# Two-layer vision kernel: image 0's first routing at earlier attention steps, routings that choose on logits, band matrices built by VectorE

## The chip, the cores and the metric

The kernel runs on one core of one Trainium2 chip. The metric is the time of the device in microseconds (us) for the whole program. A core has five engines that run their own queues in order: TensorE (PE, with its weight loads as PEld), VectorE (DVE), ScalarE (ACT), GpSimd (POOL) and SyncE (SP), which here only issues DMAs. They meet through semaphores.

## The reference

Two images of 48 x 48 tokens with 128 channels go through two layers. What the change touches are the two routings and one convolution:

```
# layer 0
x = x + window_attention(ln_c(x))        # 8 heads, windows of 4x4 queries, 8x8 keys
t = ln_t(tokens(x))
probs = softmax(t @ router_w.T)          # 8 experts
rw, re = top_k(probs, 2); rw = rw / max(sum(rw), 1e-12)
t = t + (t + sum_e combine[:, e] * (gelu(t @ w1[e] + b1[e]) @ w2[e] + b2[e]))
# layer 1
h = group_norm(conv1x1(ln_c(x)))         # 32 channels
y  = conv over channels, 9 taps (2..8 masked in) ; y2 = depthwise 9x9 conv, central 7x7
z = relu(group_norm(y + y2)); z = relu(group_norm(conv1x1(z))) + input
t = ln_t(tokens(z)); probs = softmax(t @ gate_w + gate_b)   # 16 experts
top 2 normalised by their sum; out = t_in + sum of the two experts' silu(x w1) * (x w2) @ w3
```

Because the two chosen probabilities are divided by their sum, the gates are 1 / (1 + e) and e / (1 + e), with e the exponential of second minus first logit.

## The kernel before

Each image is 18 tiles of 128 tokens, in six groups of three. One list, `order`, is written by hand, and every engine runs from it, in its order, the phases that it has a part in (`run`). `beside(kind, first, last, pieces)` lays a loop of steps and puts pieces behind numbered steps ("marks"); pieces of one mark stand in the order of the list given.

**Attention** is `("A", n)` for n from 0 to 55: 48 half window rows (24 per image) and eight steps to drain the pipeline. In step n PE makes the scores of n + 1 (line 671), transposes the probabilities of n - 3 (682), weighs n - 4 (695) and, in odd steps, projects n - 6 (706). VectorE adds the bias and takes maxima of n (1215, 1217) and sums of n - 1 (1221, 1225); GpSimd subtracts maxima of n (580), normalises n - 2 (589) and spreads queries of n + 2 (571); ScalarE takes the exponential of n - 1 (971), copies transposed probabilities of n - 3 (982) and outputs (990, 995). Behind marks stand the attended groups of each image (`YA`: transposed by PE on line 325, added by VectorE on line 1237; `YS`: their statistics), and image 0's first routing: `LN`, `SQ`, `LV` (statistics, square root, coefficients), six groups `LT` normalised by ScalarE (947), six groups `RT` transposed by PE and evacuated by ScalarE (953), `LG` logits (733), `RC` the choice in pieces 0 to 5 on VectorE, `RE` an exponential on ScalarE, `RX` the combine rows (PE 766, VectorE 1329). Inside attention all of `YA`, `RT`, `LG`, `RX` use bank 0 in turn: each waits until the one before is read.

After attention `TO` runs on GpSimd: 12 products that spread the 9x9 taps into matrices (549), 13 small operations for the channel taps (552 to 560). SyncE stores the combine rows to DRAM, reads them back, and broadcasts them as gates, four experts of a group at a time (lines 464 to 475).

**The dense layer** 0 is `("D", n)`, n from 0 to 99: 12 groups x 8 experts. Step n is a hidden product on PE (781), gelu on ScalarE (1021), the product with the gate on GpSimd (615) and, four steps later, the second product on PE (798). The second half also holds image 0's layer 1 convolution, taps on line 902, for which the matrices must be there from mark 71.

**Layer 1 routings** `RC` with l = 1 are in the list behind the logits of each image. VectorE subtracts the maximum (1263, 1264), ScalarE takes the exponential (1013), VectorE normalises (1274 to 1276), chooses twice (1280 to 1286). Then PE multiplies the chosen flags by a triangular and an all-ones matrix (810, 811), VectorE computes each token's slot (`slots`, 1358 to 1395), and GpSimd scatters the rows, 36 indirect DMAs per image (632). `moe(0)` works 20 tiles of 128 rows of image 0, `moe(1)` the other 68, after image 1's scatter (827, 836, 847). `KW` are matmuls only for the PE clock (867).

## Time and profile before

| | us |
|---|---|
| median of 3 runs (lowest to highest) | 683.85 (678.06 to 684.36) |
| the profiled execution | 683.36 |
| its span | 681.3 |
| PE busy, share | 554.9, 81% |
| VectorE | 348.6, 51% |
| ScalarE | 342.1, 50% |
| GpSimd | 408.2, 60% |
| mean granted TensorE clock | 0.905 |

The chain that ended last is 56% PE, 14% VectorE, 9% GpSimd, 9% issue, 7% ScalarE and 3% DMA. Times in the rows further down are from the start of the span. Attention runs from about 50 to 185 us, the dense layer to about 380, convolution and routings to 510, the experts of layer 1 to 658, the last sums and stores to the end. A mean over all this says little on a change to one stage: what ends a wait in that stage has to be read there.

### The profile page before, as it was taken

The numbers are of one execution on the slowest core, as the hardware profiler recorded it, in microseconds if no ns is written. First come the engines' busy times: TensorE is split into PE (matmuls) and PEld (weight loads), VectorE is DVE, ScalarE is ACT, GpSimd is POOL, SyncE is SP. The second block draws the span as 40 slices with busy tenths as digits, with TensorE's granted clock in tenths as the row PEclk, the third lists the DMA queues.
The fourth block names the chain that finished last, engine by engine and source line by source line (L and its number), as shares of the span: only waits on it lengthen the run. The fifth ranks groups of instructions, "written<-read, shape, count | busy, mean of one in ns | idle before, by whom it ended". The sixth has DMA issues, their size and how long they took to land.

```text
span 681.3 us, 15719 instructions
## 1 busy us (share of the span) xinstructions
PE 554.9 (81%) x5422; PEld 468.6 (69%) x5423; DVE 348.6 (51%) x1021; ACT 342.1 (50%) x801; POOL 408.2 (60%) x468
## 2 busy tenths in 40 slices
PE   2477788778779999999999999959649729999960
PEld 2466667657547777677777678748639729999960
DVE  6977787846620171212001274784875405555563
ACT  4467668886547243674122552522515406666640
POOL 1568789767567388675333330037747777777771
PEclk9689999979869699999999988978978959999995
DMA  8452322212055455322219200001123123333457
GB/s 296 161 140 82 85 73 81 67 47 70 13 180 201 154 174 171 128 94 99 88 47 331 61 1 1 0 23 52 52 61 98 52 85 99 98 97 98 128 204 242
DMA packets 56288, 72.15 MB, mean 106 GB/s; under 512 B 9086, under 2 KB 46934, under 8 KB 55614
## 3 DMA queue, kind: packets, MB, share of 16 engines
q1 hardware_dynamic: 49374, 58.36, 27.5%
q0 software_dynamic: 5120, 10.57, 4.7%
q10 hardware_dynamic: 1728, 2.36, 0.9%
q8 instruction: 39, 0.64, 0.4%
q14 instruction: 27, 0.22, 0.1%
HBM read 55.83 MB, written 21.69 MB: 114 GB/s over the span
## 4 chain that ended last, share of the span: by engine, by line
PE 56%; DVE 14%; POOL 9%; issue 9%; ACT 7%; DMA 3%; SPq 1%; POOLq 0%; DVEq 0%; ACTq 0%
PE bank L836 12%; PE bank L798 9%; PE bank L781 8%; PE bank L902 7%; PE bank L847 6%; POOL gathered_or_att L580 3%; POOL padded_or_w L571 3%; ACT normed L947 2%; POOL gathered_or_att L589 2%; PE bank L325 2%; DVE ln_stats L1133 2%; PE bank L796 2%; PE bank L827 2%; PE bank L733 2%; PE bank L867 1%
## 5 line engine op out<-in xcount | busy, mean ns | idle before, releaser
L615 POOL TENSOR_TENSOR padded_or_w<-padded_or_w,gathered_or_att 128x384 f32<-128x384 f32 x96 | 95.4, 1000 | 80.7 <-ACT padded_or_w L1021 77.0
L632 POOL DMA_INDIRECT sorted_x<-normed,slot x72 | 71.2, 989 | 80.0 <-DVE slot L1395 51.4
L1021 ACT ACTIVATE padded_or_w<-bank,moe_b 128x384 f32<-128x384 f32 x96 | 55.3, 579 | 107.2 <-PE bank L781 107.1
L651 POOL DMA_INDIRECT returned<-gathered_or_att,home_of_slot x88 | 87.2, 991 | 26.8 <-issue 19.8
L798 PEld LDWEIGHTS bank<-moe_or_conv,padded_or_w 128*128 128x128 f32 x576 | 80.6, 197 | 30.9 <-issue 9.8
L798 PE MATMUL bank<-moe_or_conv,padded_or_w 128*128 128x128 f32 x576 | 83.9, 284 | 0.0
L781 PE MATMUL bank<-chan_major,moe_or_conv 128*128 128x384 f32 x192 | 82.7, 517 | 0.1
L671 PE MATMUL bank<-padded_or_w 64*64 64x64 f32 x1152 | 47.5, 233 | 27.3 <-issue 15.9
L1459 DVE TENSOR_TENSOR att_or_moe<-att_or_moe,bank 128x256 f32<-128x256 f32 x88 | 37.0, 420 | 61.2 <-ACT att_or_moe L1035 39.9
L671 PEld LDWEIGHTS bank<-padded_or_w 64*64 64x64 f32 x1152 | 41.5, 145 | 36.6 <-issue 32.8
L580 POOL TENSOR_TENSOR gathered_or_att<-gathered_or_att,score_max 128x384 f32<-128x384 f32 x48 | 39.9, 830 | 34.5 <-DVE score_max L1217 33.7
L1035 ACT ACTIVATE att_or_moe<-bank 128x256 f32<-128x256 f32 x88 | 33.7, 383 | 50.7 <-PE bank L836 50.7
L1342 DVE TENSOR_TENSOR residual<-residual,bank 128x384 f32<-128x384 f32 x12 | 6.6, 552 | 98.6 <-PE bank L798 98.6
L982 ACT ACTIVATE gathered_or_att<-bank 64x384 f32<-64x384 f32 x96 | 46.2, 481 | 19.9 <-PE bank L682 19.3
L836 PE MATMUL bank<-att_or_moe,chan_major 128*128 128x128 f32 x352 | 50.0, 288 | 6.3 <-DVE chan_major L1451 6.3
L847 PE MATMUL bank<-w,att_or_moe 128*128 x352 | 53.5, 276 | 0.9 <-ACT gathered_or_att L1044 0.9
L836 PEld LDWEIGHTS bank<-att_or_moe,chan_major 128*128 128x128 f32 x352 | 46.1, 204 | 6.5 <-issue 6.5
L571 POOL TENSOR_TENSOR padded_or_w<-qy,consts 128x384 f32<-128x384 f32 x48 | 39.7, 828 | 16.1 <-ACT qy L964 16.1
L947 ACT ACTIVATE normed<-residual,ln_values 128x128 f32<-128x128 f32 x117 | 47.6, 483 | 1.5 <-DVE ln_values L1156 1.4
L847 PEld LDWEIGHTS bank<-w,att_or_moe 128*128 128x128 f32 x352 | 46.2, 192 | 1.3 <-issue 1.3
L836 PE MATMUL bank<-chan_major 128*128 128x128 f32 x352 | 46.8, 276 | 0.0
L1451 DVE COPY chan_major<-padded_or_w 128x512 f32 x88 | 38.1, 437 | 15.6 <-PE bank L836 13.6
(214 smaller groups left out, 1122.8 us busy)
## 6 DMA issues: line engine op xcount, KB each, us to landing
gathered_or_att<-combine SPq DMA_DIRECT2D x24, 768.0 KB, 4.2
padded_or_w<-windows SPq DMA_DIRECT2D x192, 48.0 KB, 2.0
sorted_x<-in_pad_rows SPq DMA_DIRECT2D x22, 260.0 KB, 7.1
padded_or_w<-sorted_x SPq DMA_DIRECT2D x22, 260.0 KB
padded_or_w<-in_moe_w SPq DMA_DIRECT2D x8, 512.0 KB, 5.4
qy<-returned SPq DMA_DIRECT2D x6, 384.0 KB, 5.8
out<-residual ACTq DMA_DIRECT2D x12, 192.0 KB, 2.1
normed<-returned SPq DMA_DIRECT2D x6, 384.0 KB, 5.4
```

The costliest lines, as they stand in the source:

```text
L571: nc.gpsimd.tensor_tensor(out_, of_step(QY[b], row, n % 2).unsqueeze(2).broadcast_to([P, HW_, HEADS // 2, Q]), HM.unsqueeze(1).unsqueeze(3 ...
L580: nc.gpsimd.tensor_tensor(sb_, sb_, MXS[:, hf, :].unsqueeze(2).broadcast_to([P, HW_, KEYS]), ALU.subtract).then_inc(S("shifted"), 1)
L615: nc.gpsimd.tensor_tensor(HB[n % DRING], HB[n % DRING], GB_[k % 3][:, n % 4, :], ALU.mult).then_inc(S("gated"), 1)
L632: nc.gpsimd.indirect_dma_start(xs_dram, bass.IndirectOffsetOnAxis(ap=POS[b][:, k, t:t + 1], axis=0), TNR[b][:, t, :], None).then_inc(S(don ...
L651: nc.gpsimd.indirect_dma_start(yt_dram, bass.IndirectOffsetOnAxis(ap=HOMES[b][:, j:j + 1], axis=0), YR[k * RING + j % RING], None).then_in ...
L671: ins = nc.tensor.matmul(banks[2 + hf][m, w * KEYS:(w + 1) * KEYS], QBD[n % 4][m, w, :], KG[b][m, row:row + 2, k0:k0 + 2 * Q], start=True, ...
L781: nc.tensor.matmul(banks[HBANK[n % 2]][:, 0:DG], W1E[:, e, :], CM[b][:, g * DG:(g + 1) * DG], start=True, stop=True).then_inc(S("h_full"), 1)
L798: ins = nc.tensor.matmul(acc[:, t * P:(t + 1) * P], HB[n % DRING][:, t * P:(t + 1) * P], W2E[:, e, :], start=False, stop=(e == EX[0] - 1 a ...
L836: ins = nc.tensor.matmul(banks[2 + r % 2][:, a * P:(a + 1) * P], W12S[r][:, a, :], XTS[r][:, :], start=True, stop=True)
L847: ins = nc.tensor.matmul(banks[6 + r % 2][:, 0:P], HID[r][:, a * P:(a + 1) * P], W3[:, ds(e, 1), a, :], start=(a == 0), stop=(a == 1))
L947: ins = nc.scalar.activation(TN[b][:, t, :], XT[b][:, t, :], ACT.Identity, bias=lv[:, 6, t:t + 1], scale=lv[:, 5, t:t + 1])
L1021: nc.scalar.activation(HB[n % DRING], banks[HBANK[n % 2]][:, 0:DG], ACT.Gelu, bias=B1C[:, e:e + 1]).then_inc(S("gelu"), 1)
```

## The change

1. Image 0's first routing moves from marks 34 to 53 to marks 33 to 48 of attention: statistics and coefficients all behind step 33, the normalise groups two per step, the transposes one per step, the logits at 41, the combine rows at 48.
2. All four routings choose on the logits (in layer 0 shifted by the maximum). The exponential is of the difference of the two chosen, 18 columns, in a tile of its own. In layer 1 ScalarE runs it between the third and the fourth normalise group.
3. The slots scan the all-ones product where PE leaves it, which reads the flags transposed; the triangular matrix has ones subtracted (`TRO`), so that the running sum needs no subtraction.
4. The matrices for the taps are built by VectorE, 20 pieces at marks 28 to 47 of the dense layer's first half; GpSimd keeps four small operations after attention. Three constants are made ahead of `centre_gate` at mark 40.

```diff
-            (34, ("LN", "LR", 0, 0)), (34, ("SQ", "LR", 0, 0)), (35, ("LV", "LR", 0, 0)), *every(36, 1, groups("LT", "LR", 0, 0)),
-            *every(37, 1.5, groups("RT", 0, 0)), (46, ("LG", 0, 0)), (47, ("RC", 0, 0, 0)), (47, ("RE", 0, 0)), *every(48, 1, choice(0, 0, 1, 6)),
-            (53, ("RX", 0)), *every(36, 4, groups("YA", 1)[:5]), *every(37, 4, groups("YS", 1)[:5])])
+            (33, ("LN", "LR", 0, 0)), (33, ("SQ", "LR", 0, 0)), (33, ("LV", "LR", 0, 0)), *every(34, .5, groups("LT", "LR", 0, 0)),
+            *every(35, 1, groups("RT", 0, 0)), (41, ("LG", 0, 0)), (42, ("RC", 0, 0, 0)), *every(43, 1, choice(0, 0, 2, 4)), (44, ("RE", 0, 0)), *every(45, 1, choice(0, 0, 4, 6)),
+            (48, ("RX", 0)), *every(36, 4, groups("YA", 1)[:5]), *every(37, 4, groups("YS", 1)[:5])])
...
-            *every(2, 4, groups("AN", "LR", 0, 0)), (19, ("LG", 0, 1)), (20, ("RC", 0, 1, 0)), (21, ("RE", 0, 1)), *every(22, 1, choice(0, 1, 1, 6)),
-            (33, ("RX", 1)), (40, ("GC", 0)), *every(28, 4, groups("AN", "LR", 0, 1))])
+            *every(2, 4, groups("AN", "LR", 0, 0)), (19, ("LG", 0, 1)), (20, ("RC", 0, 1, 0)), *every(21, 1, choice(0, 1, 2, 4)), (23, ("RE", 0, 1)), *every(24, 1, choice(0, 1, 4, 6)),
+            (33, ("RX", 1)), *every(28, 1, [("TP", k) for k in range(KA * 4 + 8)]), (40, ("GC", 0)), *every(28, 4, groups("AN", "LR", 0, 1))])
...
-                  *normed("LR", 1, 0)[:3], ("RC", 1, 0, 0), ("RE", 1, 0), *groups("LT", "LR", 1, 0), *choice(1, 0, 1, 6), *taps(1, 15, 42), ("RP", 0), *taps(1, 42, 54),
+                  *normed("LR", 1, 0)[:3], *groups("LT", "LR", 1, 0)[:3], ("RE", 1, 0), *groups("LT", "LR", 1, 0)[3:], ("RC", 1, 0, 0), *choice(1, 0, 1, 6), *taps(1, 15, 42), ("RP", 0), *taps(1, 42, 54),
...
-                pool.wait_ge(S("small_in"), 16 * 7)
-                for a in range(KA):
-                    for r in range(4):
-                        nc.gpsimd.tensor_tensor(TOEP[:, a * KX:(a + 1) * KX, 32 * r:32 * r + 32], I32.unsqueeze(1).broadcast_to([P, KX, 32]),
-                                                W2R[:, 4 * a - r + 3, :].unsqueeze(2).broadcast_to([P, KX, 32]), ALU.mult)
-
-                nc.gpsimd.tensor_scalar(BAND[:, :], DJ[:, 0:32], W1C[:, 1:2], None, ALU.mult).then_inc(S("band"), 1)
-                for j in range(1, 7):
-                    nc.gpsimd.tensor_scalar(BND[:, :], DJ[:, 32 * j:32 * j + 32], W1C[:, j + 1:j + 2], None, ALU.mult).then_inc(S("band"), 1)
-                    pool.wait_ge(S("band"), 2 * j)
-                    nc.gpsimd.tensor_tensor(BAND[:, :], BAND[:, :], BND[:, :], ALU.add).then_inc(S("band"), 1)
-                    pool.wait_ge(S("band"), 2 * j + 1)
-                for r in range(4):
-                    blk = TOEP[32 * r:32 * r + 32, KX + KX // 2, 32 * r:32 * r + 32]
-                    nc.gpsimd.tensor_tensor(blk, blk, BAND[32 * r:32 * r + 32, :], ALU.add).then_inc(S("toeplitz"), 1)
...
-                nc.tensor.matmul(banks[6][:, 0:TT * E], TRI, RT[:, 5, 0:TT * E], start=True, stop=True)
-                nc.tensor.matmul(banks[7][:, 0:TT * E], ONE, RT[:, 5, 0:TT * E], start=True, stop=True).then_inc(S("prefix"), 1)
+                nc.tensor.matmul(banks[7][:, 0:TT * E], ONE, RT[:, 5, 0:TT * E].rearrange("p (t e) -> p e t", e=E), start=True, stop=True)
+                nc.tensor.matmul(banks[6][:, 0:TT * E], TRO[:, :], RT[:, 5, 0:TT * E], start=True, stop=True).then_inc(S("prefix"), 1)
...
-            def logit_exp(l, b):
-                if l == 0:
-                    t_wait_read(act, group_no[("LG", l, b)])
-                else:
-                    act.wait_ge(S("logit_shift"), b + 1)
-                nc.scalar.activation(RT[:, 1, 0:TT * EX[l]], RT[:, 0, 0:TT * EX[l]], ACT.Exp).then_inc(S("logit_exp"), 1)
+            def gap_exp(l, b):
+                n = l * NB + b
+                act.wait_ge(S("logit_gap"), n + 1)
+                nc.scalar.activation(GEXP[:, :], RV[:, 3, :], ACT.Exp).then_inc(S("gap_exp"), 1)
...
-                        link(nc.vector.tensor_reduce(v[0], row(0), AX, ALU.max))
-                        tt(row(0), row(0), over_e(v[0]), ALU.subtract).then_inc(S("logit_shift"), 1)
                         return
                     m = group_no[("LG", l, b)]
                     t_wait_full(dve, m)
                     lg = t_bank(m)[:, 0:c].rearrange("p (t e) -> p t e", e=E)
                     link(nc.vector.tensor_reduce(v[0], lg, AX, ALU.max))
                     t_read(tt(row(0), lg, over_e(v[0]), ALU.subtract), m)
-
-                if piece == 1:
-                    dve.wait_ge(S("logit_exp"), n + 1)
-                    link(nc.vector.tensor_reduce(v[0], row(1), AX, ALU.add))
-                    link(nc.vector.reciprocal(v[1], v[0]))
-                    link(tt(row(1), row(1), over_e(v[1]), ALU.mult))
+                    t_wait_read(dve, m)
 
                 if piece in (2, 3):
                     k = piece - 2
-                    link(nc.vector.tensor_reduce(v[k], row(1), AX, ALU.max))
-                    link(tt(row(0), row(1), over_e(v[k]), ALU.is_equal))
-                    link(tt(row(0), row(0), over_t(REV[:, 0:E]), ALU.mult))
-                    link(nc.vector.tensor_reduce(v[2], row(0), AX, ALU.max))
-                    link(tt(row(2 + k), row(0), over_e(v[2]), ALU.is_equal))
+                    a, same = row(0), row(1)
+                    if l == 0 and k == 0:
+                        link(nc.vector.scalar_tensor_tensor(same, a, 0.0, over_t(REV[:, 0:E]), ALU.is_ge, ALU.mult))
+                    else:
+                        link(nc.vector.tensor_reduce(v[k], a, AX, ALU.max))
+                        if k:
+                            (tt(v[3], v[1], v[0], ALU.subtract) if l else nc.vector.tensor_copy(v[3], v[1])).then_inc(S("logit_gap"), 1)
+                        link(tt(same, a, over_e(v[k]), ALU.is_equal))
+                        link(tt(same, same, over_t(REV[:, 0:E]), ALU.mult))
+                    link(nc.vector.tensor_reduce(v[2], same, AX, ALU.max))
+                    link(tt(row(2 + k), same, over_e(v[2]), ALU.is_equal))
                     if k == 0:
-                        link(nc.vector.scalar_tensor_tensor(row(1), row(2), -2.0, row(1), ALU.mult, ALU.add))
+                        link(nc.vector.scalar_tensor_tensor(a, row(2), -1e38, a, ALU.mult, ALU.add))
 
                 if piece == 4:
                     if l:
                         tt(row(5), row(2), row(3), ALU.add).then_inc(S("chosen"), 1)
-                    link(tt(v[2], v[0], v[1], ALU.add))
-                    if l == 0:
-                        link(nc.vector.tensor_scalar_max(v[2], v[2], 1e-12))
+                    dve.wait_ge(S("gap_exp"), n + 1)
+                    link(ts(v[2], GEXP[:, :], 1.0, None, ALU.add))
                     link(nc.vector.reciprocal(v[3], v[2]))
                     if l == 0:
-                        tt(GATE[b][:, 0, :], v[0], v[3], ALU.mult)
-                        link(tt(GATE[b][:, 1, :], v[1], v[3], ALU.mult))
+                        nc.vector.tensor_copy(GATE[b][:, 0, :], v[3])
+                        link(tt(GATE[b][:, 1, :], GEXP[:, :], v[3], ALU.mult))
                     else:
                         dve.wait_ge(S("homes_set"), 2 * NB)
-                        tt(TNR[b][:, :, P + 1], v[0], v[3], ALU.mult)
-                        tt(NEXT[b][:, :, 1], v[1], v[3], ALU.mult).then_inc(S("first_gates"), 1)
+                        nc.vector.tensor_copy(TNR[b][:, :, P + 1], v[3])
+                        tt(NEXT[b][:, :, 1], GEXP[:, :], v[3], ALU.mult).then_inc(S("first_gates"), 1)
...
+            def toeplitz(piece):
+                if piece == 0:
+                    dve.wait_ge(S("small_in"), 16 * 7)
+                if piece < KA * 4:
+                    a, r = divmod(piece, 4)
+                    link(tt(TOEP[:, a * KX:(a + 1) * KX, 32 * r:32 * r + 32], I32.unsqueeze(1).broadcast_to([P, KX, 32]),
+                            W2R[:, 4 * a - r + 3, :].unsqueeze(2).broadcast_to([P, KX, 32]), ALU.mult))
+                elif piece == KA * 4:
+                    link(ts(BAND[:, :], DJ[:, 0:32], W1C[:, 1:2], None, ALU.mult))
+                elif piece < KA * 4 + 7:
+                    j = piece - KA * 4
+                    link(nc.vector.scalar_tensor_tensor(BAND[:, :], DJ[:, 32 * j:32 * j + 32], W1C[:, j + 1:j + 2], BAND[:, :], ALU.mult, ALU.add))
+                else:
+                    for r in range(4):
+                        blk = TOEP[32 * r:32 * r + 32, KX + KX // 2, 32 * r:32 * r + 32]
+                        tt(blk, blk, BAND[32 * r:32 * r + 32, :], ALU.add).then_inc(S("toeplitz"), 1)
+
             def centre_gate(k):
                 m = group_no[("GC", k)]
+                link(nc.vector.memset(SAME[:, :], 1.0))
+                link(nc.vector.memset(SAME[:, :].rearrange("p (e t) -> p e t", t=TT)[:, :, 0:1], 0.0))
+                link(tt(TRO[:, :], TRI, ONE, ALU.subtract))
...
-                tot = RT[:, 0, 0:c].rearrange("p (e t) -> p e t", t=TT)
-                one = RT[:, 1, 0:c].rearrange("p (e t) -> p e t", t=TT)
-                nc.vector.memset(RT[:, 1, 0:c], 1.0).then_inc(S("dve_chain"), 1)
-                chain[0] += 1
-                link(nc.vector.tensor_copy(tot, banks[7][:, 0:c].rearrange("p (t e) -> p e t", e=E)))
-                link(nc.vector.memset(one[:, :, 0:1], 0.0))
-                link(nc.vector.tensor_tensor_scan(RT[:, 4, 0:c], RT[:, 1, 0:c], RT[:, 0, 0:c], 0.0, ALU.mult, ALU.add))
+                link(nc.vector.tensor_tensor_scan(RT[:, 4, 0:c], SAME[:, :], banks[7][:, 0:c], 0.0, ALU.mult, ALU.add))
                 run_ = RT[:, 4, 0:c].rearrange("p (e t) -> p e t", t=TT)
                 cnt, nt, st, en = (RS[:, k, 0:E] for k in range(4))
                 over, base, delta, room, first_c, ids = (JS[:, k, 0:E] for k in range(6))
                 tmp = RT[:, 1, 0:c].rearrange("p (e t) -> p e t", t=TT)
-                nc.vector.tensor_copy(cnt, run_[:, :, TT - 1])
-                link(tt(tot, run_, tot, ALU.subtract))
+                link(nc.vector.tensor_copy(cnt, run_[:, :, TT - 1]))
...
-                link(tt(row(4), tot.rearrange("p e t -> p t e"), banks[6][:, 0:c].rearrange("p (t e) -> p t e", e=E), ALU.add))
-                link(tt(row(1), row(4), over_t(room), ALU.is_ge))
+                link(tt(row(0), run_.rearrange("p e t -> p t e"), banks[6][:, 0:c].rearrange("p (t e) -> p t e", e=E), ALU.add))
+                link(tt(row(1), row(0), over_t(room), ALU.is_ge))
                 link(tt(row(1), row(1), over_t(delta), ALU.mult))
-                link(tt(row(4), row(4), over_t(base), ALU.add))
+                link(tt(row(4), row(0), over_t(base), ALU.add))
```

## Rows read from the trace of the kernel before

**Rows 1.** Windows of three stretches, busy us and instruction counts of each engine
```profile
core 0: us, PE busy (x) PEld busy (x) DVE busy (x) ACT busy (x) POOL busy (x), PEclk, DMA share, GB/s
100.00:110.00 10.00, 9.01 (x217) 7.57 (x215) 7.83 (x21) 8.22 (x18) 9.46 (x13) 1.00 0.32 88
140.00:147.00 7.00, 3.63 (x103) 2.93 (x103) 2.49 (x6) 6.90 (x18) 3.87 (x5) 0.92 0.19 53
...
198.00:204.00 6.00, 6.00 (x18) 4.13 (x19) 0.00 (x0) 1.90 (x5) 5.47 (x6) 0.51 0.53 191
```

**Rows 2.** Timeline of VectorE: start, us, line, operation; steps 34, 41, 47
```profile
122.14 0.56 DVE L1215 TENSOR_TENSOR gathered_or_att<-bank,pos_bias 128x384 f32<-128x384 f32 x1
...
148.38 0.55 DVE L1215 TENSOR_TENSOR gathered_or_att<-bank,pos_bias 128x384 f32<-128x384 f32 x1
...
166.69 0.53 DVE L1215 TENSOR_TENSOR gathered_or_att<-bank,pos_bias 128x384 f32<-128x384 f32 x1
```

**Rows 3.** Timeline of PE, same columns, the idle time before a row in brackets
```profile
166.92 5.32 PE L733 MATMUL bank<-router_w,chan_major 128*128 128x8 f32 x36
...
184.48 0.89 PE L706 MATMUL bank<-att_or_moe,out_w_parity 128*128 128x192 f32 x4 [0.47 <-ACT qy L995]
...
189.48 5.63 PE L781 MATMUL bank<-chan_major,moe_or_conv 128*128 128x384 f32 x10
```

**Rows 4.** Chain of waits between attention and dense layer: start, us, what
```profile
190.11 1.45 DMA combine<-att_or_moe
...
191.95 4.73 DMA gathered_or_att<-combine
...
197.88 1.64 PE bank L796 x2
```

**Rows 5.** Timeline of PE, two waits of layer 1
```profile
452.04 0.35 PE L875 MATMUL bank<-gn_values,consts 128*128 128x2 f32 x2 [4.31 <-DVE gn_values L1499]
...
556.97 0.45 PE L827 MATMUL bank<-consts,padded_or_w 128*128 128x128 f32 x1 [15.17 <-issue]
```

**Rows 6.** Timeline of VectorE: image 0's slots, image 1's choice
```profile
440.64 0.30 DVE L1358 MEMSET route<- 128x288 f32 x1 [2.94 <-PE bank L811]
...
441.44 0.76 DVE L1362 TENSOR_TENSOR_SCAN route<-route 128x288 f32<-128x288 f32 x1
...
442.81 0.17 DVE L1371 TENSOR_SCALAR joint_tiles<-route_small 128x16 f32<-128x16 f32 x1
...
484.70 0.45 DVE L1263 TENSOR_REDUCE route_rows<-route 128x18 f32<-128x288 f32 x1
...
487.47 0.45 DVE L1280 TENSOR_REDUCE route_rows<-route 128x18 f32<-128x288 f32 x1
```

**Rows 7.** Timeline of GpSimd: end of band matrices, dense products, second scatter's start
```profile
192.44 1.24 POOL L560 TENSOR_TENSOR toeplitz<-toeplitz,band 32x32 f32<-32x32 f32 x4
...
242.33 6.04 POOL L615 TENSOR_TENSOR padded_or_w<-padded_or_w,gathered_or_att 128x384 f32<-128x384 f32 x6
...
505.53 0.97 POOL L632 DMA_INDIRECT sorted_x<-normed,slot  x1 [7.39 <-issue]
```

**Rows 8.** Timeline of ScalarE in attention steps 34 to 37
```profile
126.38 0.22 ACT L934 ACTIVATE ln_values<-ln_values 128x18 f32<-128x18 f32 x1 [0.99 <-DVE ln_values L1150]
...
127.91 0.52 ACT L971 ACTIVATE gathered_or_att<-gathered_or_att 128x384 f32<-128x384 f32 x1
...
129.73 0.52 ACT L971 ACTIVATE gathered_or_att<-gathered_or_att 128x384 f32<-128x384 f32 x1
...
131.91 1.25 ACT L947 ACTIVATE normed<-residual,ln_values 128x128 f32<-128x128 f32 x3
...
136.15 0.49 ACT L953 ACTIVATE chan_major<-bank 128x384 f32<-128x384 f32 x1
```

**Rows 9.** Timeline of VectorE: products with constants in layer 0's two choices
```profile
179.23 0.79 DVE L1282 TENSOR_TENSOR route<-route,consts 128x144 f32<-128x144 f32 x1
...
240.16 0.31 DVE L1282 TENSOR_TENSOR route<-route,consts 128x144 f32<-128x144 f32 x1
...
243.60 0.99 DVE L1282 TENSOR_TENSOR route<-route,consts 128x144 f32<-128x144 f32 x1
```

15 lines of the change are left out of this document (8 added, 7 removed).

## The prediction

> **What bounds the kernel now.** I read the busy time by stretch first. At 100 to 110 us, plain attention, GpSimd works 9.46 of 10 us: its three tensor operations per attention step set a step of about 2.4 to 2.5 us [rows 1]. From step 34 on this no longer holds. The step starts on VectorE (line 1215) show step 34 at 122.14, step 41 at 148.38 and step 47 at 166.69 [rows 2]: 26.2 us for seven steps, 18.3 for the next six. In 140 to 147 ScalarE is busy 6.90 of 7 us and PE 3.63 [rows 1]: ScalarE normalises and evacuates for image 0's routing, and PE and VectorE wait for bank 0, which it reads late.
>
> Then the tail. The logits hold PE from 166.92 for 5.32 us; attention's last projection ends at 185.37; hidden products of the dense layer start at 189.48 [rows 3]. The chain of waits says why its second half starts only at 197.88: combine rows stored from 190.11 (1.45 us), gates broadcast from 191.95 (4.73 us), one GpSimd product [rows 4]. So the routing is the path from the logits to 197.88. PE, idle 2.8 us before, then runs at 0.51 clock from 198 to 204 [rows 1]. From there to 400 us PE is full but for short stretches, and a shift is passed on.
>
> Later VectorE's slot calculation for image 0 is last: PE waits 4.31 us on it at 452.04 [rows 5]. Image 1's choice is last too: its scatter starts at 505.53 after GpSimd had nothing for 7.39 us, and PE stands still 15.17 us for the scattered rows until 556.97 [rows 5, 7].
>
> **Part 1, layer 1 routings.** Choosing on logits removes lines 1263 to 1276 with their wait for ScalarE: 484.70 to 487.47, 2.77 us [rows 6]. The gap difference adds 0.1 (18 elements, not linked). The choice rounds keep their twelve operations. Minus 2.67 for image 1. Image 0's choice saves the same, but it ends before PE reaches the prefix matmuls, behind its taps: nothing.
>
> In the slots, the memset, the copy and the memset before the scan (440.64 to 441.44) and the subtraction behind the copy go; of 440.64 to 442.81 stay a scan (0.79) and a copy (0.2): 1.17 saved per image [rows 6]. The scan now reads a bank; bound 0 to 0.2 more, I take 0. The all-ones matmul reads its 288 columns transposed; no row shows that stride; with 0 to 0.7 us each (288 columns at full speed take 0.25 to 0.5), I take 0. Image 0's 1.17 counts, because VectorE is last there [rows 5]; image 1's counts in the scatter's start. The first scatter, 1.17 earlier, ends at 497, before 505.53 - 5.0 = 500.5, so GpSimd doesn't bind. ScalarE's exponential of the gap sits between its normalise groups 3 and 4: nine activations from 483.3 end at 486.8, a table load follows, and the gap is there at 488.3, ahead of its use at 490.6. The scatter needs the last normalise at 492, and starts at 500. Sum: 1.17 + 2.67 + 1.17 = **5.0 us**, with 4.3 to 6.5 (PE warm at the prefix instead of at the low clock would add 1.3).
>
> **Part 2, image 0's first routing.** I walk it with before's durations. A ScalarE step is 1.8 to 2.2 us (127.91 to 129.73 to 131.91), three normalises 1.2, an evacuation 0.45 (0.49 less what overlaps) [rows 8]. A VectorE step is 1.75.
>
> - Step 33 now holds statistics, coefficients and the wait for the square root. The root comes about 1.7 us earlier than 126.38 [rows 8], and VectorE starts step 34 at 125.5, not 122.14.
> - ScalarE starts its exponential of step 33 at 126.15. Six normalise groups lie in steps 34 to 36, two per step, not one per step in 36 to 41: 126.15 + 3 x 2.0 + 6 x 1.2 + 2 x 0.45 gives 140.1 for the evacuation of transposes 1. The attended group of image 1 at mark 36 waits behind it in bank 0, so PE (idle some 4.5 us) and VectorE meet ScalarE there: step 37 starts at 141.5, not 132.28.
> - PE restarts at the low clock and ScalarE starves some 3.4 us. Four steps with an evacuation each bring transposes 5 to 154.4. The attended group at mark 40 waits for it again: step 41 at 155.4 against 148.38 [rows 2], 7.0 late, but with normalises and transposes all done.
> - Logits on PE from 157.3 for 5.25 [rows 3], five steps earlier than before. Then VectorE is the bound: products with constants take 0.7 while GpSimd runs [rows 9], so pieces 2, 3, 4, 5 cost 2.0, 2.2, 1.1, 1.8. With 1.75 of attention and the image 1 pieces between, steps 44 to 47 start at 168.5, 172.9, 176.3, 179.8.
> - Mark 48 copies the combine rows once step 47's sums are there, 183.5. Bank 0 makes PE wait for that. Two more projections, weighings and evacuations in turn end at 189.6, against 185.37 [rows 3]. The combine rows store at once, and the gates land at 183.5 + 2.25 + 4.73 = 190.5 [rows 4], ahead of use. The whole DMA chain is hidden.
> - Hidden products start at 190.5. Five need 3.4 us warm (0.65 each, with gelu between), not the 5.63 of [rows 3]. Second half at 193.9, instead of 197.88. Seven matmul groups after it take 3.7 to 4.0 warm against 6.6 cold [rows 1]: the dense layer is 6.5 ahead. I take off 1.2 for a dozen handoffs of 0.1 that the walk rounds away: **5.3 us**.
>
> If the clock is low there all the same, it is 1.8 - 0.6, say 1.2. Errors of the walk: 3 either way.
>
> **Part 3, band matrices.** GpSimd's 16 us from 177.8 to 193.68 [rows 7] go. Before they were hidden, as the gates landed at 196.7; at the new start they would be in the way by 3 us, so this move is needed for part 2's gain and has none of its own. VectorE gets 20 pieces in dense steps 28 to 47: twelve of 0.46 (same elements as the choice rounds) and eight small ones. It is nearly idle there; with waits for GpSimd (0.31 becomes 0.99 at worst [rows 9]) about 20 of the 26 us. What queues behind them on VectorE is the sum into the residual, every eight steps, with a step group (10 us) to spare, and the copy of image 1's combine rows. The three preparations in the centring are 1 us at a place with 6 us of idle. Cost zero; without cover 1 us each.
>
> The other side is GpSimd: a gating product of 1.0 per step and 0.95 every fourth are 1.24 of a 1.31 us step. From 242.33 on six products run 6.04 us in a row [rows 7] while VectorE does two-source operations beside them: 1.007 each, no delay. The Trainium skill ("SBUF — State Buffer", Who interferes with whom) says that a VectorE operation with two SBUF sources and a GpSimd one that reads SBUF exclude each other, and whichever starts first blocks the other for its whole instruction. VectorE's 0.99 agrees, GpSimd's 1.007 doesn't show the reverse. Were GpSimd held by each piece (a rival, below), 12 x 0.46 + 8 x 0.15 = 6.7 us of delay would meet 20 x 0.07 = 1.4 of slack and about 2.9 that the four-step lag holds: 2.4 lost.
>
> **Sum.** The profiled execution took 683.36 (span 681.3 and 2.06 outside), 0.5 below the median 683.85 of three (678.06 to 684.36). 683.36 - 5.0 - 5.3 = 673.0.
>
> **Rivals.**
>
> - *Forecast*: tail warm, gates hidden. 673, range 669.5 to 676. Chance 0.45.
> - *The attention gives it back*: the wait at mark 36, or VectorE's four long steps, costs 4 us more, or the dense layer starts at the low clock. For it: four such waits lie in 34 to 48, and PE fell to 0.51 after 2.8 us idle [rows 1, 4]. Against: PE has no idle that long ahead of the dense layer. Part 2 brings 0 to 2: 677.5. Chance 0.27.
> - *The burst costs less*: normalises ahead of need let PE and VectorE run on, and step 41 comes 3 to 4 us earlier. Part 2 brings 9: 669. Chance 0.12.
> - *GpSimd is held by VectorE's pieces* (dense steps 28 to 47): 2.4 on top: 675.5. Chance 0.08. The Trainium skill's page named above gives the reason.
> - *The low clock stays* (the slower side). PE idles 4.5 us at mark 36 and is then about half busy. If the clock stays low until the dense layer has run six us, PE's step is 3.7 instead of 2.1: some 1 us more in each of four steps, 0.6 in six VectorE-bound ones, 3 in the tail, 4.6 at the dense start [rows 1]: 15 in all, less 1 of overlap: 673 + 14 = 687. It decides from 10.3 us of such loss. Against: before fell at 147 and was back within 5 us. Chance 0.05.
> - *The moves do nothing*: DMA for the gates still ends last, or the second saving is hidden by the first scatter. Only part of the 5.0 is left: 680. Against: GpSimd's idle of 7.39 [rows 7]. Chance 0.03.
>
> Range: from the burst case to above the give-back case, 668 to 680.5; this leaves out the low clock and some of each end. A measurement of this kernel tells about 1% (6.8 us) from no change: faster means under 677. Of the forecast's 0.45 I count 0.43 as faster, of burst 0.12, of held 0.05, of give-back 0.06: 0.66. Slower (over 690.7) are the low clock with a longer stay than priced, and mishaps no row shows: 0.05. Same: 0.29.
>
> **What would show it.** Step 37 near 141 and step 41 near 155 on line 1215; logits from about 157; combine stored before attention's last projection; second-half products within 5 us of the first hidden one, granted clock 1.00. Slots 1.17 shorter; PE's stand before the second group of tiles still 15 us, because everything before it moves too. Wrong if step 47 comes after 184, if the gelu table wait or gates stand ahead of the dense products, or if GpSimd's product exceeds 1.1 us beside the band pieces.

## The result

| | median us | lowest to highest | executions | mean |
|---|---|---|---|---|
| before | 684.01 | 678.06 to 689.90 | 20 | 683.8 |
| changed | 680.07 | 672.25 to 682.77 | 20 | 679.0 |

The changed kernel takes 0.9942 of the time, with a 95% interval of 0.9917 to 0.9967: 3.9 us less, where 10.8 was forecast. The ratio leaves out executions more than 1.5% above the fastest; over all of them the means differ by 4.8 us. The changed kernel's profiled execution took 676.86 us (span 675.0) against 683.36, so this pair of traces shows more than the medians do.

What the forecast said one would see is there. VectorE's step starts (line 1199 now, same columns as [rows 2]), steps 34, 37, 41 and 47, forecast at 125.5, 141.5, 155.4 and 179.8:

```profile
124.60 0.55 DVE L1199 TENSOR_TENSOR gathered_or_att<-bank,pos_bias 128x384 f32<-128x384 f32 x1
...
140.59 0.55 DVE L1199 TENSOR_TENSOR gathered_or_att<-bank,pos_bias 128x384 f32<-128x384 f32 x1
...
154.14 0.55 DVE L1199 TENSOR_TENSOR gathered_or_att<-bank,pos_bias 128x384 f32<-128x384 f32 x1
...
177.43 0.55 DVE L1199 TENSOR_TENSOR gathered_or_att<-bank,pos_bias 128x384 f32<-128x384 f32 x1
```

PE (against [rows 3], and the first of the dense layer's second products, those behind the gates, line 782, against 197.88 in [rows 4]): logits, last projection, hidden products, second products. As in the forecast, these second products are called the "second half" from here on.

```profile
155.86 4.18 PE L719 MATMUL bank<-router_w,chan_major 128*128 128x8 f32 x36
...
189.45 0.89 PE L692 MATMUL bank<-att_or_moe,out_w_parity 128*128 128x192 f32 x4 [0.46 <-ACT qy L981]
...
191.20 3.98 PE L767 MATMUL bank<-chan_major,moe_or_conv 128*128 128x384 f32 x10
195.11 0.91 PE L782 MATMUL bank<-moe_b,att_or_moe 24*128 24x384 f32 x2
```

The combine rows leave from SP at 181.34 and the gates' broadcast at 183.57 (SP's rows of the timeline), under attention's last steps:

```profile
181.34 0.35 SPq L466 DMA_DIRECT2D combine<-att_or_moe  x1
...
183.57 14.44 SPq L477 DMA_DIRECT2D gathered_or_att<-combine  x4
```

And the second half starts warm: the window from 196 us has a granted clock of 1.00 where [rows 1] show 0.51.

```profile
core 0: us, PE busy (x) PEld busy (x) DVE busy (x) ACT busy (x) POOL busy (x), PEclk, DMA share, GB/s
...
196.00:202.00 6.00, 5.31 (x35) 4.32 (x35) 1.33 (x3) 5.17 (x11) 4.56 (x6) 1.00 0.50 176
```

In layer 1, PE's wait of [rows 5] for image 0's slots is 3.04 us instead of 4.31, the second scatter starts at 499.77 instead of 505.53 [rows 7], and PE still stands 14.76 us ahead of the second tiles (timelines of PE and GpSimd):

```profile
449.38 0.35 PE L861 MATMUL bank<-gn_values,consts 128*128 128x2 f32 x2 [3.04 <-DVE gn_values L1494]
...
550.98 0.45 PE L813 MATMUL bank<-consts,padded_or_w 128*128 128x128 f32 x1 [14.76 <-issue]
```

```profile
494.49 0.97 POOL L618 DMA_INDIRECT sorted_x<-normed,slot  x1 [0.30 <-issue]
499.77 0.97 POOL L618 DMA_INDIRECT sorted_x<-normed,slot  x1 [4.31 <-issue]
```

The pair also invites a wrong story. At the hidden product of dense step 28 the changed kernel is 7.2 us ahead (238.65 against 245.84), at image 1's first convolution tap only 1.85 (408.64 against 410.49). The windows show PE at 1.2 GHz, the lower of its two levels, behind a wait of 1.54 us that both kernels have. Changed kernel:

```profile
377.65 0.75 PE L903 MATMUL bank<-conv_mid,conv_w 32*128 32x288 f32 x2 [1.54 <-ACT conv_mid L1075]
```

```profile
376.00:382.00 6.00, 4.46 (x18) 2.90 (x18) 0.11 (x1) 2.60 (x6) 1.95 (x2) 0.79 0.00 0
382.00:388.00 6.00, 6.00 (x20) 4.26 (x21) 2.72 (x14) 2.50 (x4) 0.75 (x1) 0.50 0.00 0
```

The kernel before, the same wait and the windows behind it:

```profile
384.84 0.75 PE L917 MATMUL bank<-conv_mid,conv_w 32*128 32x288 f32 x2 [1.54 <-ACT conv_mid L1091]
```

```profile
382.00:388.00 6.00, 4.46 (x29) 3.25 (x27) 1.27 (x6) 3.78 (x7) 1.95 (x2) 1.00 0.00 0
388.00:394.00 6.00, 6.00 (x44) 5.11 (x45) 3.90 (x20) 3.20 (x6) 0.75 (x1) 1.00 0.00 0
```

It looks as if the change made the clock fall and lost 5.3 us by it. The first experiments are about that.

### The profile page after: what moved, and what is told of

The parts are those of the page before. It is cut to its first block, busy times and chain, and to the rows that moved or that the text cites. A ratio compares the mean times of both kernels' runs of the same rounds, so it can differ in the third digit from the quotient of the medians.

```text
span 675.0 us, 15692 instructions
## 1 busy us (share of the span) xinstructions
PE 559.1 (83%) x5422; PEld 472.2 (70%) x5423; DVE 357.4 (53%) x1021; ACT 341.7 (51%) x801; POOL 396.0 (59%) x439
## 3 DMA queue, kind: packets, MB, share of 16 engines
q1 hardware_dynamic: 49374, 58.36, 27.5%
## 4 chain that ended last, share of the span: by engine, by line
PE 59%; DVE 11%; issue 9%; POOL 8%; ACT 8%; DMA 3%; SPq 2%; POOLq 0%; DVEq 0%; ACTq 0%
PE bank L822 12%; PE bank L784 9%; PE bank L767 8%; PE bank L888 7%; PE bank L833 6%; POOL gathered_or_att L566 3%; ACT normed L933 3%; PE bank L853 3%; POOL padded_or_w L557 2%; PE bank L657 2%; POOL gathered_or_att L575 2%; PE bank L903 2%; PE bank L327 2%; DVE ln_stats L1117 2%; PE bank L813 2%
## 5 line engine op out<-in xcount | busy, mean ns | idle before, releaser
L637 POOL DMA_INDIRECT returned<-gathered_or_att,home_of_slot x88 | 87.0, 989 | 26.8 <-issue 20.7
L767 PE MATMUL bank<-chan_major,moe_or_conv 128*128 128x384 f32 x192 | 79.1, 495 | 1.5 <-ACT padded_or_w L1005 1.5
L657 PE MATMUL bank<-padded_or_w 64*64 64x64 f32 x1152 | 49.5, 239 | 25.1 <-issue 14.3
L657 PEld LDWEIGHTS bank<-padded_or_w 64*64 64x64 f32 x1152 | 43.2, 151 | 35.2 <-issue 35.2
L566 POOL TENSOR_TENSOR gathered_or_att<-gathered_or_att,score_max 128x384 f32<-128x384 f32 x48 | 39.9, 830 | 44.3 <-DVE score_max L1201 39.8
L822 PEld LDWEIGHTS bank<-att_or_moe,chan_major 128*128 128x128 f32 x352 | 46.1, 204 | 3.3 <-issue 3.3
```

The source lines that it names most:

```text
L566: nc.gpsimd.tensor_tensor(sb_, sb_, MXS[:, hf, :].unsqueeze(2).broadcast_to([P, HW_, KEYS]), ALU.subtract).then_inc(S("shifted"), 1)
L637: nc.gpsimd.indirect_dma_start(yt_dram, bass.IndirectOffsetOnAxis(ap=HOMES[b][:, j:j + 1], axis=0), YR[k * RING + j % RING], None).then_in ...
L657: ins = nc.tensor.matmul(banks[2 + hf][m, w * KEYS:(w + 1) * KEYS], QBD[n % 4][m, w, :], KG[b][m, row:row + 2, k0:k0 + 2 * Q], start=True, ...
L767: nc.tensor.matmul(banks[HBANK[n % 2]][:, 0:DG], W1E[:, e, :], CM[b][:, g * DG:(g + 1) * DG], start=True, stop=True).then_inc(S("h_full"), 1)
L822: ins = nc.tensor.matmul(banks[2 + r % 2][:, a * P:(a + 1) * P], W12S[r][:, a, :], XTS[r][:, :], start=True, stop=True)
```

## Experiments: is the clock part of the change?

**The same kernels again.** Each kernel was profiled twice more, unaltered.

> The changed kernel once more, unaltered, for a second trace of the same instructions. Theory A (PE's clock falls at places that are liable to it, but in one execution and not in the next): the low stretch of 10.2 us behind the 1.54 us wait of the first up-projection (377.65 in the first trace) is there or not, and the low stretch behind image 1's logits (3.4 us in the first trace, 10.2 us in the variant with extra products, which has the same instructions up to there) has another length; time from first hidden product to step 28's between 47.4 and 50.8 us; whole time within 672 to 683. Rival E (the falls belong to the program): the same stretches as in the first trace, 10.2 us at 379.5 and 3.4 us at 225.9, and 47.4 us between the hidden products, within 1 us.

> A third trace of the changed kernel, as the second. Theory A: at least two of the three traces differ by 3 us or more somewhere between 190 and 410 us. Rival E: all three alike within 1 us.

> The kernel before once more, unaltered. In its first trace no low stretch lay between 238 and 398 us, though PE stood 1.54 us at 384.84. Theory A: the fall of 10.2 us behind that wait appears in some of its executions too, and its time lies anywhere from 679 to 691. Rival E: again none there, and 29.0 us from the last hidden product to image 1's first tap (34.4 in the changed kernel).

> A third trace of the kernel before, as the second. Theory A: at least two of the three differ by 3 us or more between 190 and 410 us. Rival E: all three alike within 1 us.

682.02, 678.83, 685.86 and 689.23 us. Second trace of the kernel before (PE, then windows):

```profile
379.03 0.75 PE L917 MATMUL bank<-conv_mid,conv_w 32*128 32x288 f32 x2 [1.55 <-ACT conv_mid L1091]
```

```profile
382.00:388.00 6.00, 6.00 (x17) 3.70 (x16) 1.01 (x4) 1.00 (x2) 0.75 (x1) 0.50 0.00 0
388.00:394.00 6.00, 6.00 (x30) 5.93 (x30) 5.44 (x21) 5.25 (x12) 2.27 (x3) 0.54 0.00 0
```

So it falls there too; the first trace of before was the lucky one. Theory A holds for whether a fall comes and for its length. Times between landmarks (read from the timelines; step 0 is attention's first step on VectorE, "second half" the first of the second products with an expert's weights, line 798 or 784; hidden 28 and 95 the hidden products of these dense steps; "LN logits" line 1260 or 1244, image 1's gate logits; the first tiles' weight product line 836 or 822):

| stretch, us | before x3 | mean | changed x3 | mean | difference |
|---|---|---|---|---|---|
| step 0 to second half | 175.3, 171.1, 174.5 | 173.6 | 172.4, 175.5, 172.1 | 173.3 | -0.3 |
| second half to hidden 28 | 46.4, 45.6, 46.4 | 46.1 | 42.7, 44.3, 44.3 | 43.8 | -2.3 |
| hidden 28 to 95 | 135.6 each | 135.6 | 135.6 each | 135.6 | 0 |
| hidden 95 to image 1's first tap | 29.0, 37.9, 38.2 | 35.0 | 34.4, 36.3, 34.4 | 35.0 | 0 |
| image 0's prefix products to LN logits | 43.9, 43.7, 43.4 | 43.7 | 43.8, 43.2, 43.8 | 43.6 | -0.1 |
| LN logits to the first tiles' weight product | 26.9, 26.9, 26.8 | 26.9 | 23.1, 23.1, 23.0 | 23.0 | -3.8 |
| from there to the end | 171.2, 171.3, 170.6 | 171.1 | 170.7, 170.4, 171.3 | 170.8 | -0.3 |

The same instructions differ by up to 9.2 us in one stretch and by 0.1 in another; the loss at the dense layer's end is none of the change's. What is stable is the -3.8 in layer 1. Its two ends, in the first trace of the kernel before and then of the changed kernel (timelines of VectorE and PE):

```profile
483.24 0.45 DVE L1260 TENSOR_TENSOR route<-logits_of_norm,bank 128x288 f32<-128x288 f32 x1
510.12 2.05 PE L836 MATMUL bank<-att_or_moe,chan_major 128*128 128x128 f32 x8 [6.28 <-DVE chan_major L1451]
```

```profile
481.26 0.45 DVE L1244 TENSOR_TENSOR route<-logits_of_norm,bank 128x288 f32<-128x288 f32 x1
504.36 2.04 PE L822 MATMUL bank<-att_or_moe,chan_major 128*128 128x128 f32 x8 [2.98 <-DVE chan_major L1446]
```

The -2.3 ahead of hidden 28 is less solid. Image 1's logits of layer 0 are followed by a stretch at the low clock. It lasted 10.2 us in all three traces of before and 3.4, 6.8 and 6.8 in the changed kernel's. But it also lasted 10.2 in the next variant, whose instructions are the changed kernel's up to there. From these logits to hidden 28 it is 20.8, 20.5 and 20.5 us in before and 18.2, 19.9 and 19.9 in the changed kernel, so 1.2 of the 2.3 lies behind that stretch.

**Clock kept up at that wait.**

```diff
-            *every(96, 1, [("XU", 0, n) for n in range(4)])])
+            (96, ("KW", 12, "gelu", DN)), *every(96, 1, [("XU", 0, n) for n in range(4)])])
```

> The changed kernel with one thing more: twelve idle-filling products on PE ahead of image 0's first up-projection, where PE stood 1.54 us for the middle convolution's output at 377.65. In the changed kernel's trace the granted clock fell to 0.50 at 379.49 for 10.24 us behind that wait; before it stayed at 1.00 behind the same wait. Theory A (that wait lets the clock fall in some executions): no low clock between 375 and 395, PE's work there 5 us shorter where it would have fallen, median 676 to 678. Rival C (the low clock there has nothing to do with the wait): median 680, with the products' own 0 to 0.5 us on top.

678.44 us, ratio 0.9935 (0.9894 to 0.9976), not told from the change's 0.9942. No low stretch at 380; hidden 95 to the first tap took 31.8 us instead of 34.4. But PE fell at 422.4 for 6.8 us behind many small gate products, where none of the six traces above does. That costs 3.3 us; it came in 5 of the 11 variants' traces, and its cause stays open.

## Experiments: which part brings what

**One part alone.** choice_alone is the changed kernel with the old steps (diff below, at late_marks) and `TO=toeplitz` on GpSimd again. moves_alone is the kernel before with the new steps and with `TP` on VectorE; its choice keeps the five old pieces, `*every(43, 1, choice(0, 0, 1, 6))`.

> The kernel before with part 1 alone: both layers choose on logits, slots shortened; image 0's first routing stays at steps 34 to 53, band matrices stay on GpSimd. Theory A (clock falls give back what the earlier routing won; part 1 keeps its gain of 3.55 us, which is what the second tiles' start gained on the first slot pieces in the two traces): 684.0 - 3.6 = 680.4, and no difference beyond 0.5 us in the dense layer. Rival B (the earlier routing keeps its gain and the shorter slots and choice are lost behind something else): 684. Forecast of the prediction: 684.0 - 5.0 = 679.

> The kernel before with image 0's first routing at steps 33 to 48 and the band matrices on VectorE, but choice and slots as before (so the choice has its five old pieces, at steps 43 to 47). Theory A: ahead in the dense layer by 4 to 7 us, and most of it gone again between the dense layer's end and the second image's convolution; 684.0 - 1.5 = 682.5. Rival B: 684.0 - 3.9 = 680. Forecast of the prediction: 684.0 - 5.3 = 678.7.

choice_alone: 681.51, ratio 0.9970 (0.9933 to 1.0008). moves_alone: 684.89, ratio 1.0055 (1.0027 to 1.0083). Over all executions the means are 680.1 and 684.5, against 685.6 for before beside them: 5.5 and 1.1 us less. So the earlier routing and the matrices on VectorE, without the shorter choice, bring nothing that can be told, and none of the three theories had that (682.5, 680, 678.7). In the trace of moves_alone attention's last projection ends at 193.06, against 183.83 in choice_alone's.

**Band matrices back on GpSimd, the rest as changed.** GpSimd's old `toeplitz` runs at `TO` again:

```diff
-            (33, ("RX", 1)), *every(28, 1, [("TP", k) for k in range(KA * 4 + 8)]), (40, ("GC", 0)), *every(28, 4, groups("AN", "LR", 0, 1))])
+            (33, ("RX", 1)), (40, ("GC", 0)), *every(28, 4, groups("AN", "LR", 0, 1))])
```

> The changed kernel with the band matrices back on GpSimd ahead of the dense layer (16 us there). Theory A and the prediction: GpSimd ends them at about 193.7, the gates' product waits for it, and the dense layer's second half starts 1 to 3 us later than in the changed kernel: 681 to 683. Rival D (VectorE's pieces hold GpSimd in dense steps 28 to 47): the changed kernel loses 2.4 us there, and this one is as fast or faster: 678 to 680.

684.18, ratio 1.0029 (0.9992 to 1.0066). GpSimd ends the bands at 197.65 and takes the gates' product right behind:

```profile
196.44 1.21 POOL L563 TENSOR_TENSOR toeplitz<-toeplitz,band 32x32 f32<-32x32 f32 x4
197.73 2.89 POOL L618 TENSOR_TENSOR padded_or_w<-padded_or_w,gathered_or_att 128x384 f32<-128x384 f32 x3
```

Step 0 to second half is 176.8 us, 3.5 more than the changed kernel's mean. Rival D falls; the time is 1 us above what theory A gave. The edit also leaves band_gpsimd and choice_alone with the steps as their only difference, and they ran beside each other: means of 684.6 and 680.1 over 12 executions each. With the matrices on GpSimd the new steps cost 4.5 us.

**Old steps for image 0's routing, the rest as changed.**

```diff
-            (33, ("LN", "LR", 0, 0)), (33, ("SQ", "LR", 0, 0)), (33, ("LV", "LR", 0, 0)), *every(34, .5, groups("LT", "LR", 0, 0)),
-            *every(35, 1, groups("RT", 0, 0)), (41, ("LG", 0, 0)), (42, ("RC", 0, 0, 0)), *every(43, 1, choice(0, 0, 2, 4)), (44, ("RE", 0, 0)), *every(45, 1, choice(0, 0, 4, 6)),
-            (48, ("RX", 0)),
+            (34, ("LN", "LR", 0, 0)), (34, ("SQ", "LR", 0, 0)), (35, ("LV", "LR", 0, 0)), *every(36, 1, groups("LT", "LR", 0, 0)),
+            *every(37, 1.5, groups("RT", 0, 0)), (46, ("LG", 0, 0)), (47, ("RC", 0, 0, 0)), *every(49, 1, choice(0, 0, 2, 4)), (50, ("RE", 0, 0)), *every(51, 1, choice(0, 0, 4, 6)),
+            (53, ("RX", 0)),
```

> The changed kernel with image 0's first routing back at its old steps (statistics at 34, transposes from 37, logits at 46, combine rows at 53); the choice on logits and the band matrices on VectorE stay. Theory G (moving the routing forward brings nothing where the choice is already short, because attention ends 7.8 us later for it in the mean of the traces): 680 to 682, with attention's last projection near 184, the first hidden product near 185.5, and the dense layer's second half waiting for the gates until 194 to 195. Prediction's theory (the move is worth 5.3): 684 to 685.

678.42, ratio 0.9938 (0.9903 to 0.9974): the same as the change. The move that the forecast priced at 5.3 us brings nothing that can be told. Its timeline of PE:

```profile
164.67 4.18 PE L719 MATMUL bank<-router_w,chan_major 128*128 128x8 f32 x36
...
180.89 0.89 PE L692 MATMUL bank<-att_or_moe,out_w_parity 128*128 128x192 f32 x4 [0.47 <-ACT qy L981]
190.12 1.64 PE L782 MATMUL bank<-moe_b,att_or_moe 24*128 24x384 f32 x2 [3.50 <-POOL padded_or_w L601]
```

The logits are 8.8 us later than in the changed kernel and the last projection 8.6 earlier. The gates are waited for, from a combine DMA of 1.45 us at 183.06 and a broadcast of 4.04 at 184.89, and still the second half starts 5 us before the changed kernel's in this pair of traces, more than theory G gave it (5.3 before its mean, measured from step 0 to line 784). The lead doesn't last: from there to hidden 28 this trace takes 47.1 us, the changed kernel's 42.7 to 44.3. It has 14.6 us of that at the low clock, part of it behind the 3.50 us wait for the gates, and they have 3.4 to 6.8.

**Six normalise groups, one per step.**

```diff
-            (33, ("LN", "LR", 0, 0)), (33, ("SQ", "LR", 0, 0)), (33, ("LV", "LR", 0, 0)), *every(34, .5, groups("LT", "LR", 0, 0)),
-            *every(35, 1, groups("RT", 0, 0)), (41, ("LG", 0, 0)), (42, ("RC", 0, 0, 0)), *every(43, 1, choice(0, 0, 2, 4)), (44, ("RE", 0, 0)), *every(45, 1, choice(0, 0, 4, 6)),
-            (48, ("RX", 0)),
+            (33, ("LN", "LR", 0, 0)), (33, ("SQ", "LR", 0, 0)), (33, ("LV", "LR", 0, 0)), *every(34, 1, groups("LT", "LR", 0, 0)),
+            *every(35, 1, groups("RT", 0, 0)), (42, ("LG", 0, 0)), (43, ("RC", 0, 0, 0)), *every(44, 1, choice(0, 0, 2, 4)), (45, ("RE", 0, 0)), *every(46, 1, choice(0, 0, 4, 6)),
+            (49, ("RX", 0)),
```

> The changed kernel with the six normalise groups of image 0's first routing one per attention step (34 to 39) instead of two, transposes 35 to 40, logits at 42, combine rows at 49. Theory H (the burst of normalise groups is what stalls PE at step 36 and costs attention 3 to 4 us): step 37 near 136 instead of 140.6 to 141.3, attention's last projection 2 to 4 us earlier than the changed kernel's 189.9 to 193.3, time 677 to 679. Rival J (ScalarE's sum of work decides, not its spread): last projection within 1 us of the changed kernel's, time 680.

679.25, ratio 0.9934 (0.9900 to 0.9969). Step 37 starts at 138.56 (changed 140.6 to 141.3), the last projection ends at 192.62 (changed 189.9 to 193.3). The burst delays step 37 by 2 us and the end by nothing: rival J.

**The choice behind step 47.** These three build on short_early, a version of the next section. choice_late differs from it by

```diff
-            *every(35, 1, groups("RT", 0, 0)), (41, ("LG", 0, 0)), (42, ("RC", 0, 0, 0)), *every(43, 1, choice(0, 0, 2, 4)), (44, ("RE", 0, 0)), *every(45, 1, choice(0, 0, 4, 6)),
-            (48, ("RX", 0)),
+            *every(35, 1, groups("RT", 0, 0)), (41, ("LG", 0, 0)), (42, ("RC", 0, 0, 0)), *every(48, 1, choice(0, 0, 2, 4)), (49, ("RE", 0, 0)), *every(50, 1, choice(0, 0, 4, 6)),
+            (51, ("RX", 0)),
```

late_short by the old steps as in late_marks, and late_tight from that by the choice at 48 to 51 and `(51, ("RX", 0))`.

> short_early with the normalise groups, transposes and logits at the new steps (34 to 41), but the choice's pieces at 48 to 51 and the combine rows at 51. Theory M (work put among full steps displaces attention one for one): step 47 starts 5 to 6 us earlier than the changed kernel's 177.4 to 181.4, at about 172.5, attention's last projection at 184 to 186, second half at 193 to 195; the whole as short_early within 1.5 us, 672 to 674. Rival N (choice pieces beside full steps are hidden, and only the burst costs): step 47 within 2 us of the changed kernel's, and the second half later than 196: 675 to 677.

> short_early (8 and 12 clock-keeping products in place of 30 and 24, twelve ahead of image 0's first up-projection, scan released by the all-ones product) with image 0's first routing at the old steps 34 to 53. Theory G (the move is worth nothing): within 1.5 us of short_early, 672 to 674; first hidden product near 182.6, second half's first product near 190 to 192, behind the gates' DMA. Prediction's theory (the move is worth 5): 678.

> late_short with the choice's pieces one step earlier (48 to 51, not 49 to 52) and the combine rows at 51, not 53. If combine rows and gates' DMA (1.45 and 4.0 us in late_marks' chain) are the path there: dense layer's second half 1 to 2 us earlier than late_short, 671 to 673. If attention is delayed by as much as the gates come earlier: as late_short.

| variant | median us | ratio (95%) | step 47 | last projection ends | second half |
|---|---|---|---|---|---|
| short_early | 673.10 | 0.9861 (0.9813 to 0.9910) | 176.61 | 188.44 | 194.06 |
| choice_late | 670.72 | 0.9838 (0.9797 to 0.9878) | 173.94 | 188.11 | 195.13 |
| late_short | 675.08 | 0.9910 (0.9876 to 0.9945) | 167.29 | 185.49 | 195.20 |
| late_tight | 671.92 | 0.9845 (0.9802 to 0.9888) | 167.37 | 188.08 | 194.68 |

Step 47 comes 9 us apart, the second half 1.1 us apart. Every interval overlaps short_early's; those of choice_late and late_short only touch. Each row is one trace, and by hidden 28 the four are up to 3.6 us apart again (238.4, 241.8, 238.3 and 240.2). Neither M nor N is met whole: step 47 moved by 2.7 us, less than M's 5, and the last projection not at all. late_short was forecast at 672 to 674 with the second half at 190 to 192, and missed both. late_tight has the time it was given, but its second half is only 0.5 us earlier and its last projection 2.6 later, which is the other theory. What holds is the common part: where a routing piece is put between step 33 and the end of attention changes when steps run, and hardly when they all are done.

## Experiments: where image 0's shorter slots went

The slots are shorter. From VectorE's first operation on them to the product of the group statistics behind them it is 11.40 us in before and 10.22 in the changed kernel: 1.18 less, as forecast. But VectorE starts them 1.65 us behind the first prefix product, not 1.26, because the all-ones product with its transposed read takes 1.13 us for its two records and the other, of the same width but read straight, 0.66. From the first prefix product on it is 12.66 us in each trace of before and 11.88 in each of the changed kernel, 0.78 less:

```profile
437.51 1.13 PE L796 MATMUL bank<-route,consts 128*128 128x288 f32 x2
438.46 0.66 PE L797 MATMUL bank<-route,not_before 128*128 128x288 f32 x2
```

By the LN logits 0.1 of the 0.78 is left. Timeline of PE in the changed kernel; then VectorE, whose input for the product of line 861 is ready at 462.66:

```profile
458.92 9.76 PE L853 MATMUL bank<-consts 128*128 128x128 f32 x60 [0.59 <-ACT chan_major L1083]
468.52 0.28 PE L861 MATMUL bank<-gn_values,consts 128*128 128x2 f32 x2
```

```profile
462.50 0.16 DVE L1494 TENSOR_TENSOR gn_values<-gn_values 128x1 f32<-128x1 f32 x1
468.84 0.16 DVE L1496 COPY gn_values<-bank 128x2 f32<-128x2 f32 x1 [6.18 <-PE bank L861]
```

Line 853 is the product that only keeps the clock up, 30 times. It holds the path for 5.9 us. And it takes longer: with the 10 behind it 11.4 to 11.8 us in before, 12.0 to 12.3 in the changed kernel. By the granted clock PE is at 1.2 GHz for their first 5.1 us in the one and 5.9 in the other: started earlier, they lie longer in the low stretch.

```diff
-("GN", "XU", 1), ("KW", 30, "up_out", 8 * NB), ("GS", "XU", 1),
+("GN", "XU", 1), ("KW", 8, "up_out", 8 * NB), ("GS", "XU", 1),
```

> The changed kernel with one number altered: 8 instead of 30 clock-keeping products on PE ahead of the group statistics of image 1's up-projection. In the changed kernel's trace VectorE has those statistics' input at 462.66, and PE's product for them starts at 468.41, behind 80 records of such products. Theory K (these products are on the path, so image 0's shorter slots are swallowed there, as the products then run longer at the low clock: 12.2 us against 11.4 to 11.8): the gain of 0.8 comes back and 4 to 5 us more with it, until GpSimd's first scatter (ends 495.5) holds the second, 675.5 to 676.5. Rival L (without them the clock is low for image 1's logits and group statistics, which costs as much): 679 to 681.

678.50, ratio 0.9888 (0.9842 to 0.9934); mean of all 677.0 against 679.0. The median is in neither theory's range. Prefix products to LN logits: 40.0 us instead of 43.6, and then 25.1 instead of 23.0 to the first tiles' weight product, so 2.1 of the 3.6 are given back. Rival L has a share: in the window from 465 us the clock is still 0.50, in the changed kernel 1.00 (windows, short_hold and then the changed kernel), and the 10 products behind take 4.62 us instead of 2.48.

```profile
465.00:470.00 5.00, 4.90 (x24) 4.63 (x22) 2.69 (x14) 1.16 (x3) 3.78 (x5) 0.50 0.18 57
```

```profile
465.00:470.00 5.00, 5.00 (x47) 5.00 (x47) 0.79 (x5) 0.20 (x1) 3.78 (x5) 1.00 0.17 53
```

The other limit is new: GpSimd has become the bound of the second scatter, whose first row (500.17) now follows the last of the first scatter without a gap:

```profile
498.89 0.97 POOL L618 DMA_INDIRECT sorted_x<-normed,slot  x1 [0.30 <-issue]
500.17 0.97 POOL L618 DMA_INDIRECT sorted_x<-normed,slot  x1 [0.30 <-issue]
```

**The same, with three more edits.**

> As short_hold, and: 12 instead of 24 clock-keeping products behind the dense layer, twelve such products ahead of image 0's first up-projection, and the scan of the slots released by the all-ones product alone (prefix count 2b + 1), the other prefix product only ahead of the sum that reads it. The scan starts 0.5 to 0.7 us earlier behind the prefix products in both images (1.65 us in the changed kernel), the low stretch of 10.2 us near 380 is absent or shorter. Theory: short_hold's gain and 1 to 4 us more, 672 to 675. Rival (clock falls move elsewhere, as in the variant with the twelve products alone, where a stretch of 6.8 us came at 422): as short_hold.

```diff
-                nc.tensor.matmul(banks[7][:, 0:TT * E], ONE, RT[:, 5, 0:TT * E].rearrange("p (t e) -> p e t", e=E), start=True, stop=True)
+                nc.tensor.matmul(banks[7][:, 0:TT * E], ONE, RT[:, 5, 0:TT * E].rearrange("p (t e) -> p e t", e=E), start=True, stop=True).then_inc(S("prefix"), 1)
-                dve.wait_ge(S("prefix"), b + 1)
+                dve.wait_ge(S("prefix"), 2 * b + 1)
...
+                dve.wait_ge(S("prefix"), 2 * b + 2)
                 link(tt(row(0), run_.rearrange("p e t -> p t e"), banks[6][:, 0:c].rearrange("p (t e) -> p t e", e=E), ALU.add))
```

673.10 us, 0.9861 (0.9813 to 0.9910). The scan starts 1.17 us behind the first prefix product instead of 1.65, prefix products to LN logits take 37.4 us, and no low stretch lies at 380; a shorter one, of 6.8 us, lies at 391. Not all of the 6.2 us gained ahead of the LN logits stays: from them to the end it is 196.7 us instead of 193.8, because image 1's first slots are there at 488.0 and GpSimd is busy with the first scatter until 493. With the choice's pieces moved (choice_late above) it is 670.72 us, 0.9838 of before. Its interval and short_early's lie below the change's: these versions beat both kernels.

## Why the prediction was wrong

**Part 2, the step that failed: "Second half at 193.9, instead of 197.88", the lead of 4.0 us with which the dense layer was to start.** The walk through attention was near. In three traces steps 34, 37 and 41 came within 1.7 us, step 47 at 177.4, 181.4 and 178.1 for 179.8, the end of the last projection at 190.3, 193.3 and 189.9 for 189.6, gates hidden, second half warm. The lead failed by what it was compared with, and by 2 us of the walk. Line 782 came at 195.1, 198.0 and 194.7, in the mean 2.0 later than 193.9. And the 197.88 of [rows 4] is one execution, and a late one. From step 0 to the first second product (line 796 or 782) it is 173.8, 170.2 and 172.9 us in before, 171.5, 174.7 and 171.2 in the changed kernel: 172.3 and 172.5 in the mean, no lead at all.

The other term was the warm start, 6.5 less 4.0: 2.5 us. It is there and smaller. From that product to image 1's logits it is 25.3 us in each trace of the changed kernel and 27.2, 26.0 and 27.5 in before: 1.6 us. Another 1.2 come behind these logits, from low stretches that were shorter in these three traces and not in keep_clock_97's: luck, as far as the traces tell. Together 2.7 us of the 5.3 are left by hidden 28.

The moved steps were also never priced against the old steps with the shorter choice and a free GpSimd. That kernel (late_marks) is at hidden 28 215.1 us behind step 0, late_short, with the same instructions up to there, 214.6, the changed one 215.1, 219.9 and 216.4. So the lead is that of the shorter choice and of the gates' product that no longer waits for bands; the steps add nothing. In the forecast's words: the tail collapsed as said, and attention paid for it.

**Part 1: 5.0 forecast, 3.9 measured.** Image 1's choice and slots were 3.84 and came out at 3.8. PE is at the low clock there in both kernels, and the transposed read costs nothing (488.80 in the changed kernel: 1.33 us, the straight one at 493.38 in before 1.32). In image 0, at the high clock, it cost 0.4, inside its bound of 0 to 0.7 where I took 0. Image 0's 1.17 counted "because VectorE is last there". It is, for the wait in [rows 5]; the next one, six microseconds on, belongs to PE's clock-keeping products, and the chain was not followed that far. Short_hold shows that they are the path. So 0.1 is left of the 1.17.

**Part 3: zero, and right.** Hidden 28 to hidden 48, with the pieces on VectorE beside it, takes 29.85 us in before and in the changed kernel. The pieces were sized too small: the twelve take 1.01 us in the mean, not 0.46, beside GpSimd's products. Of the 20 products there, 16 stay at 0.99 to 1.07 and four take 1.12 to 1.23, in each trace of the changed kernel, where band_gpsimd's are all at 0.99 to 1.01. So one sign that was set for "wrong", a product above 1.1 us, was met, and cost no time.

```profile
239.98 5.15 DVE L1296 TENSOR_TENSOR toeplitz<-consts,conv_rows 128x288 f32<-128x288 f32 x5
```

```profile
243.82 1.00 POOL L601 TENSOR_TENSOR padded_or_w<-padded_or_w,gathered_or_att 128x384 f32<-128x384 f32 x1 [0.25 <-ACT padded_or_w L1005]
245.13 0.99 POOL L601 TENSOR_TENSOR padded_or_w<-padded_or_w,gathered_or_att 128x384 f32<-128x384 f32 x1 [0.32 <-ACT padded_or_w L1005]
```

VectorE pays, GpSimd hardly. The Trainium skill's rule ("SBUF — State Buffer", Who interferes with whom) has whichever starts first block the other. The trace agrees for VectorE's side, with pieces of 0.44 us alone and 1.0 to 1.2 beside the products, and for GpSimd's only in those four, by up to 0.23 us. That the bands would be 3 us in the way on GpSimd is confirmed by band_gpsimd at 3.5. "Before they were hidden" holds for the kernel before alone: once the choice is short, they are in the way at the old steps too, where choice_alone is at hidden 28 218.8 us behind step 0 and late_marks 215.1 (one trace each; in the times the two are not told apart).

**Rivals.** "The attention gives it back" (677.5, chance 0.27) named the right place and nearly the number: with Part 1's 1.1 us short it gives 678.6, and the mean is 679.0. That is partly luck, because its mechanism, waits that cost 4 us more than walked or a start at the low clock, is not what happened. GpSimd held: refuted. The low clock staying through attention: refuted, 4.75 us from first hidden product to second half in each trace. Two readings in the walk were slightly off without bearing on this: its own terms give 140.25 for the 140.1, and the low stretch of before at 147 lasted from 145.8 to 152.6.

**Sum.** The spans of three traces each differ by 6.7 us (684.1 and 677.4 in the mean); 20 executions give -4.8 in the mean and -3.9 by the ratio. Three draws of something that spreads by 10 us allow that; how often a fall comes at 422, and how long the one behind image 1's logits lasts, is left open.

## What to carry to other kernels

Before pricing a moved piece, price the same kernel with the piece where it was: here, among steps whose engines are all near full, moved work delayed the steps by about as much as it arrived earlier (8.6 us for 8.8). When the time saved ends at a wait, follow the chain to the next two, and count products that only keep a clock up as work in the queue: ask what stands behind them. And profile the kernel before two or three times: a stretch that differs by 9 us between executions of the same instructions can't carry a term of 5.

## What the runs showed of the hardware

- The same wait of 1.54 us stands in 12 traces. In nine PE's clock fell to 1.2 GHz within 3 us behind it, for 10.2 to 13.7 us, and in three (before, moves_alone, one_per_step) it did not.
- It also fell, for 3.4 to 10.2 us, in all 17 traces during image 1's layer 0 logits or within 1.6 us behind them (18 products of 8 columns, 36 records), though PE had stood for nothing in the 5 us before.
- At 2.4 GHz a product that reads its 288 moving columns transposed takes 1.13 us for 0.66; at 1.2 GHz it takes 1.33, and one of the same width read straight 1.32.
- With 22 clock-keeping products fewer (short_hold) the low stretch around 460 us lasted 17.1 us instead of 13.7; with as few it lasted 17.1 in late_short too, and 10.2 in short_early, choice_late and late_tight.
